# A message-passing layer on one core: filters made in one pass by PE, edges in the rows, without a bias pass on ACT and without transposes

## What is computed

```python
h = jnp.maximum(_layernorm(x, axis=-1), 0.0)
W = silu(dist_feat @ fw1 + fb1) @ fw2 + fb2      # one row of filters per edge
xt = silu(h @ aw1 + ab1) @ aw2 + ab2             # one row per node
msg = W * xt[src]
agg = jax.ops.segment_sum(msg, dst, num_segments=h.shape[0])
out = silu(agg @ ow1 + ob1) @ ow2 + ob2
return x + h + out
```

## Time and profile before

| | us |
|---|---|
| median of 3 runs | 2037.55 (2035.7 to 2040.6) |
| span of the profiled execution | 2356.9 |
| PE, DVE busy in it | 1290.8, 1191.7 |
| ACT, POOL busy in it | 520.7, 1526.1 |
| mean granted clock of PE | 0.741 of 2.4 GHz |

### The profile page before, as it was taken

The page is one execution under the profiler, slowest core; times in us unless marked ns, Lnnn a source line. Parts: engine busy times, 40 slices in busy tenths (PEclk is TensorE's granted clock), DMA queues, the critical chain, the costliest instruction groups (busy, mean ns, idle before and its releaser), DMA issues.

```text
span 2356.9 us, 13198 instructions
## 1 busy us (share of the span) xinstructions
PE 1290.8 (55%) x4526; PEld 700.7 (30%) x4526; DVE 1191.7 (51%) x1497; ACT 520.7 (22%) x545; POOL 1526.1 (65%) x1619
## 2 busy tenths in 40 slices
PE   3454555655565557555655565555564566554645
PEld 2222333332232323223322232222232233322323
DVE  4455445555455445544544564445444454444545
ACT  3322222222121122122212221222121122121211
POOL 5556666667666666666666666666666676666665
PEclk9686777777786768776877786777686777677867
DMA  4421222212221212212212221222221222212211
GB/s 148 144 76 45 82 58 71 79 51 85 82 83 45 83 50 81 87 46 81 86 51 78 80 85 50 80 65 65 82 85 48 82 54 81 85 45 82 59 46 44
DMA packets 62293, 171.47 MB, mean 73 GB/s; under 512 B 27088, under 2 KB 29648, under 8 KB 59024
## 3 DMA queue, kind: packets, MB, share of 16 engines
q0 software_dynamic: 51584, 105.75, 16.8%
q1 hardware_dynamic: 8192, 61.32, 6.9%
q10 hardware_dynamic: 2448, 3.54, 0.4%
HBM read 164.08 MB, written 6.42 MB: 72 GB/s over the span
## 4 chain that ended last, share of the span: by engine, by line
another core or an unknown queue 30%; POOL 24%; PE 18%; issue 16%; ACT 9%; DVE 2%; DMA 0%; SPq 0%; POOLq 0%; ACTq 0%; DVEq 0%
POOL xg L381 24%; PE banks L884 9%; PE banks L876 4%; ACT hid L444 4%; ACT hid L450 4%; PE banks L891 2%; PE banks L824 1%; PE banks L899 1%; ACT hs L469 0%; DVE stats L557 0%; PE banks L819 0%; DMA xs<-in_x 0%; PE banks L944 0%; DVE sums L668 0%
## 5 line engine op out<-in xcount | busy, mean ns | idle before, releaser
L381 POOL DMA_INDIRECT xg<-node_table,src x1564 | 1479.0, 946 | 777.6 <-issue 451.3
L884 PE MATMUL banks<-hid,wts 128*128 128x512 f32 x806 | 534.4, 798 | 556.3 <-ACT hid L444 437.9
L665 DVE TENSOR_TENSOR banks<-banks,xg 128x1024 f32<-128x1024 f32 (+1 forms) x198 | 241.4, 1219 | 1070.2 <-DMA xg<-node_table,src 607.2
L668 DVE TENSOR_REDUCE sums<-banks 128x128 f32<-128x1024 f32 (+1 forms) x408 | 494.0, 1211 | 13.7
L876 PE MATMUL banks<-attr,wts 50*128 50x512 f32 x806 | 284.4, 786 | 383.1 <-ACT hid L450 206.4
L444 ACT ACTIVATE hid<-banks,cols 128x1024 f32<-128x1024 f32 x202 | 224.7, 1112 | 887.9 <-remote 672.4
L450 ACT ACTIVATE hid<-banks,cols 128x1024 f32<-128x1024 f32 x202 | 224.6, 1112 | 865.6 <-remote 376.6
L884 PEld LDWEIGHTS banks<-hid,wts 128*128 128x128 f32 x806 | 180.6, 249 | 746.6 <-ACT hid L444 465.7
L891 PE MATMUL banks<-ident,hid 128*128 128x128 f32 x1612 | 283.5, 333 | 40.1 <-issue 38.1
L891 PEld LDWEIGHTS banks<-ident,hid 128*128 128x128 f32 x1612 | 224.6, 170 | 237.1 <-issue 228.6
L672 DVE TENSOR_TENSOR banks<-banks,other 128x1024 f32<-128x1024 f32 (+1 forms) x204 | 248.7, 1219 | 7.0
(11 more groups left out here) (83 smaller groups left out, 282.9 us busy)
## 6 DMA issues: line engine op xcount, KB each, us to landing
attr<-in_attr SPq DMA_DIRECT2D x25, 2048.0 KB
xg<-node_table,src POOLq DMA_INDIRECT x1564
out<-res ACTq DMA_DIRECT2D x8, 256.0 KB
xs<-in_x SPq DMA_DIRECT2D x3, 512.0 KB, 6.6
node_table<-res SPq DMA_DIRECT2D x3, 512.0 KB
out<-res ACTq DMA_DIRECT2D x5, 192.0 KB
spare<-in_dst SPq DMA_DIRECT2D x1, 808.0 KB
src<-in_src SPq DMA_DIRECT2D x1, 808.0 KB
```

The costliest lines, as they stand in the source:

```text
L381: pool.indirect_dma_start(xg[:, i % XG, j, :], None, table[:, :], bass.IndirectOffsetOnAxis(ap=src[:, s * L + j:s * L + j + 1], axis=0))\
L665: dve.tensor_tensor(to, to, rows_of, ALU.mult).then_inc(signal, 1)
L668: return dve.reduce_sum(sums[:, at, m, :], of.rearrange("p j f -> p f j"), AX.X)
L884: i = pe.matmul(hid_ps[:, at], w["fw2_s"][:, :], hid[:, s % 2, at], start=True, stop=True)
```

## The change

PE makes the filters with the edges in the partitions at once: the silu result is the stationary operand, `fw2` the moving one, eight matmuls of 128 columns a pair. fb2 comes from two bf16 matmuls of 512 columns ahead of them, which spread three bf16 parts of fb2 (`fb2_rows`) over the partitions. ACT's pass L450 and the transposes are gone, and `hid_ps` is written once a pair. DVE makes the parts of fb2 at its start, ahead of the statistics; before, that was part of a branch that isn't taken with these inputs. `hidden` runs two pairs ahead (FILL = 2). PE's semaphores of the loop (three raised a turn, and those of the steps) become one, `pe_turn`, raised by the last matmul of `hidden`; whoever waited for filters, transposes or steps of a turn waits for `hidden(s + 2)`, the last thing in PE's turn s ahead of the sums and the steps. POOL waits for it too.

```diff
+FILL = 2
+def after(s):
+    return run(s + FILL)
...
                 if i >= XG:
-                    pool.wait_ge(fil_done, run(s - REACH))
+                    pool.wait_ge(pe_turn, after(s - 1))
...
             def silu_hid(s):
                 n = tiles_in(s) * P
-                act.wait_ge(hid_sum, run(s))
+                act.wait_ge(pe_turn, run(s))
...
-            def add_fb2(s):
-                n = tiles_in(s) * P
-                act.wait_ge(across, run(s))
-                act.activation(hid[:, s % 2, 0:n], hid_ps[:, 0:n], ACT.Identity, bias=cols[:, 3:4]).then_inc(biased, 1)
...
             def pair(s):
-                for a in ((0, 1) if s == 0 else (s + 1,)):
+                for a in range(FILL + 1) if s == 0 else (s + FILL,):
                     if a < PAIRS:
                         silu_hid(a)
-                        add_fb2(a)
...
+            dve.wait_ge(s_rows, 16)
+            dve.wait_ge(s_set, 1)
+            dve.tensor_copy(fb2_part[:, 0, :], rows[:, 0, :]).then_inc(s_fb2, 1)
+            dve.wait_ge(s_fb2, 1)
+            dve.tensor_tensor(fb2_rest[:, 0, :], rows[:, 0, :], fb2_part[:, 0, :], ALU.subtract).then_inc(s_fb2, 1)
...
+            for i in range(3):
+                dve.tensor_copy(fb2_rows[32 * i:32 * i + 1, :, :],
+                                fb2_part[32 * i:32 * i + 1, i:i + 1, :].to_broadcast([1, TPG, F])).then_inc(s_fb2, 1)
...
-                dve.wait_ge(fil_done, run(s))
+                dve.wait_ge(pe_turn, after(s))
...
                 if s > 0:
-                    pe.wait_ge(biased, run(s - 1))
+                    pe.wait_ge(hid_done, run(s - 1))
...
-                i.then_inc(hid_sum, 1)
+                i.then_inc(pe_turn, 1)
...
             def filters(s):
+                to, halves = fil_ps[s % 2], range(tiles_in(s) // TPG)
+                pe.wait_ge(red_done, run(s, LAG))
+                for h in halves:
+                    pe.matmul(to[:, GC * h:GC * h + GC], ones_b[:, :], fb2_rows.rearrange("p j f -> p (j f)"), start=True, stop=False)
                 pe.wait_ge(hid_done, run(s))
-                for h in range(tiles_in(s) // TPG):
-                    at = slice(GC * h, GC * h + GC)
-                    i = pe.matmul(hid_ps[:, at], w["fw2_s"][:, :], hid[:, s % 2, at], start=True, stop=True)
-                i.then_inc(across, 1)
-
-
-            def by_edge(s):
                 for j in range(tiles_in(s)):
                     at = slice(j * P, (j + 1) * P)
-                    i = pe.transpose(fil_ps[s % 2][:, at], hid[:, s % 2, at], ident[:, :])
-                i.then_inc(fil_done, 1)
+                    i = pe.matmul(to[:, at], hid[:, s % 2, at], w["fw2_s"][:, :], start=False, stop=j % TPG == TPG - 1)
+                return i
...
             def pair(s):
                 if s == 0:
-                    hidden(s)
-                    filters(s)
-                if s + 1 < PAIRS:
-                    hidden(s + 1)
+                    for a in range(FILL):
+                        hidden(a)
+                i = filters(s)
+                if s + FILL < PAIRS:
+                    hidden(s + FILL)
                 else:
-                    pe.wait_ge(biased, run(s))
-                pe.wait_ge(red_done, run(s, LAG))
-                by_edge(s)
-                if s + 1 < PAIRS:
-                    filters(s + 1)
+                    i.then_inc(pe_turn, 1)
                 for a in SUMS_AT.get(s, ()):
                     pair_sums(a)
```

More of the change, by code:

```diff
@@ L150, in table_writes, with turn_of @@
     return sum(len(transfers(i)) for i in range(c + 1))
+def turn_of(kind, n, step):
+    return TASKS[TASK_OF[kind, n]][2] + (EARLY_STEPS if kind == "early" else OUT_STEPS)[step]
 def turns(pair, task):
@@ L287, in gnn_layer @@
         e_gathered = [sem(f"e_gathered{r}") for r in range(EARLY_PAIRS)]
-        hid_sum, hid_done, across, biased, fil_done, oh_done, msg_done, masked, first_done, red_done, half_msg, half_first, half_masked, half_red, win_done, group_done = (
-            sem(n) for n in ("hid_sum", "hid_done", "across", "biased", "fil_done", "oh_done", "msg_done", "masked", "first_done", "red_done", "half_msg",
+        pe_turn, hid_done, oh_done, msg_done, masked, first_done, red_done, half_msg, half_first, half_masked, half_red, win_done, group_done = (
+            sem(n) for n in ("pe_turn", "hid_done", "oh_done", "msg_done", "masked", "first_done", "red_done", "half_msg",
                              "half_first", "half_masked", "half_red", "win_done", "group_done"))
-        n_relu, n_tr, n_hT, n_l1, n_mid, n_l2, n_rows = (
-            sem(n) for n in ("n_relu", "n_tr", "n_hT", "n_l1", "n_mid", "n_l2", "n_rows"))
+        n_relu, n_hT, n_mid, n_rows, last_l1, last_l2 = (
+            sem(n) for n in ("n_relu", "n_hT", "n_mid", "n_rows", "last_l1", "last_l2"))
         r_din, r_key, r_in, r_gat, r_l1, r_hid, r_fil, r_msg, r_one, r_win, r_add, r_taken = (
@@ L328, in pair @@
                     if s >= 2 * PART:
-                        sp.wait_ge(hid_sum, run(s - PART - 1))
+                        sp.wait_ge(pe_turn, run(s - PART - 1))
                     at = s % (2 * PART) * GC
@@ L398, in _ @@
             act.dma_start(cols[:, :], cols_t).then_inc(s_cols, 16)
-            for ahead in (s_h, s_mid, a_mid, hid_done, biased):
+            for ahead in (s_h, s_mid, a_mid, hid_done):
                 act.sem_inc(ahead, AHEAD)
@@ L463, in task @@
                     if n >= 2:
-                        act.wait_ge(n_tr, n - 1)
+                        act.wait_ge(pe_turn, after(turn_of("early", n - 2, "copied")))
                     if n == 0:
@@ L473, in task @@
                     width, bias = (GC, 1) if kind == "early" else (OUTS[n][1] * P, 2)
[L474 to L477, removed]
+                    last = kind == "out" and n == len(OUTS) - 1
+                    if last:
+                        act.wait_ge(last_l1, 1)
+                    else:
+                        act.wait_ge(pe_turn, after(turn_of(kind, n, "middle")))
+                    source = last_ps_1 if last else node_ps
                     act.activation(mid[:, 0:width], source[:, 0:width], ACT.Silu, bias=cols[:, bias:bias + 1])\
@@ L551, in _ @@
             dve.memset(fb2_rows[:, :, :], 0.0).then_inc(s_set, 1)
+            dve.wait_ge(s_rows, 16)
[3 more added lines that the diff above has]
+            dve.tensor_tensor(fb2_rest[:, 0, :], rows[:, 0, :], fb2_part[:, 0, :], ALU.subtract).then_inc(s_fb2, 1)
+            dve.wait_ge(s_fb2, 2)
+            dve.tensor_copy(fb2_part[:, 1, :], fb2_rest[:, 0, :]).then_inc(s_fb2, 1)
+            dve.wait_ge(s_fb2, 3)
+            dve.tensor_tensor(fb2_rest[:, 1, :], fb2_rest[:, 0, :], fb2_part[:, 1, :], ALU.subtract).then_inc(s_fb2, 1)
+            dve.wait_ge(s_fb2, 4)
+            dve.tensor_copy(fb2_part[:, 2, :], fb2_rest[:, 1, :]).then_inc(s_fb2, 1)
+            dve.wait_ge(s_fb2, 5)
+            for i in range(3):
+                dve.tensor_copy(fb2_rows[32 * i:32 * i + 1, :, :],
+                                fb2_part[32 * i:32 * i + 1, i:i + 1, :].to_broadcast([1, TPG, F])).then_inc(s_fb2, 1)
             for k, (first, last) in enumerate(STAT_PARTS):
@@ L733, in task @@
                 if step == "copied":
-                    dve.wait_ge(n_tr, n + 1)
+                    dve.wait_ge(pe_turn, after(turn_of(kind, n, "copied")))
                     dve.tensor_copy(hT[:, 0:GC], node_ps).then_inc(n_hT, 1)
                 elif step == "rows" and kind == "early":
-                    dve.wait_ge(n_l2, b + 1)
+                    dve.wait_ge(pe_turn, after(turn_of(kind, n, "rows")))
                     dve.tensor_tensor(e_x[:, n * TPG:(n + 1) * TPG, :], node_ps.rearrange("p (j f) -> p j f", f=F),
@@ L747, in task @@
                     if to is yc:
-                        dve.wait_ge(n_l2, b + 1)
+                        dve.wait_ge(pe_turn, after(turn_of(kind, n, "rows")))
                     dve.tensor_tensor(to, to, rows[:, 2:3, :].to_broadcast([P, tiles, F]), ALU.add).then_inc(s_xs, 1)
                     if to is xc:
-                        dve.wait_ge(n_l2, b + 1)
+                        dve.wait_ge(last_l2, 1)
                     if n >= 2:
@@ L764, in _ @@
                     dve.wait_ge(s_out[i], 16 * len(OUTS[i::2]))
[L765 to L778, removed]
                 dve.sem_inc(r_msg, 1)
@@ L810, in _, with transposes @@
         def _(pe):
-            def transposes(to, b, n_tiles, signal):
+            def transposes(to, b, n_tiles):
                 for j in range(n_tiles):
                     i = pe.transpose(to[:, j * P:(j + 1) * P], hs[:, b, j, :], ident[:, :])
-                i.then_inc(signal, 1)
+                return i
             def layer1(source, n_tiles, weights, summed):
@@ L836, in node_transposes @@
                 pe.wait_ge(s_hT, run(c, 1))
-                transposes(tr_ps, b, TILES[c], s_tr)
+                transposes(tr_ps, b, TILES[c]).then_inc(s_tr, 1)
```

(20 more changed lines are left out.)

12 lines of the change are left out of this document (5 added, 7 removed).

## The result

The changed kernel takes 2049.59 us (median of 4 runs, 2048.06 to 2051.16) where before takes 2038.88 (4 runs, 2035.7 to 2040.6): the ratio is 1.0053, with a 95% interval of 1.0039 to 1.0066. It is 10.7 us slower.

The account below looks back on a forecast made before the run. POOL's 1612 gathers at 1.25 us, 2015 us, were taken as the bound; 2037.55 us plus 12 (early pairs), 3.0 (start) and 1.1 (node stage) gave 2053.6 us, range 2036 to 2068.

Parts of the forecast that it names:

- The bound and the mechanism: Main loop: POOL's gathers every 1.25 us, 2015 us in all, bound the kernel; PE's longer chain costs only where POOL waits.
- The early pairs' term: Six early pairs, which take no gather: POOL waits 2.0 us each for PE's longer chain, 12 us (2.7 to 23).
- PE needed only the transposes there: Kernel before, early pairs: transposes at half clock take 2.25 us with POOL's release, so no wait before the change.
- PE's 3.75 us: Early pair E: time left for PE between DVE's end with pair E-2, at 16.25, and gather E+1, due at 20.0.
- gather E+2: The gather for the second pair after early pair E: adds no wait once gather E+1's has been paid.
- The start: Gather 3 waits for turn 2, behind DVE's late end with pair 0: 3.0 us lost (1.0 to 5.4).
- The node stage: DVE's extra small passes ahead of the statistics delay the table and POOL's start in the pairs: 1.1 us (0 to 2.6).
- The account of the stalls: POOL's waits in the first profile of before, 321 us, come from profiling; without the profiler POOL hardly waits.
- the rival that they are: "Faster": stalls also occur in ordinary runs and partly vanish with PE's increments, 1845 to 2018 us; chance 0.10.
- Same: Early turns: PE at full clock and a slightly shorter chain make the six waits vanish, 2037 to 2041 us; chance 0.27.
- Slower still: Ordinary turns exceed their 13.75 us for PE; a tenth of them losing 2 us each gives 2094 us; chance 0.03.
- The full price of 3.85 us an early pair: Early pairs: upper end of each wait, with PE's whole burst at half clock, 7.6 us; 23 us in all.

Follow-up runs that it names:

- The direct waits of POOL: POOL waits for DVE's end with the pair that last used the slot, not for PE: changed kernel 2030.42 us, kernel before 2030.29 us.
- the chains shortened step by step: Changed kernel with POOL released by the filters instead of hidden, 2040.21 us; changed kernel without the bias matmuls for fb2, 2044.54 us.
- the run with two more increments: Changed kernel plus two more PE semaphore increments a turn that nobody waits for, three a turn as before: 2046.34 us, ratio 1.0048.
- the second profile of before: The kernel before, unchanged, profiled again: one run, 2036.49 us, with a span of 2034.7 us.

## Why the prediction held, and where it was off

**The bound and the mechanism: right.** POOL's spacing of 1.25 us is the clock of this kernel, ordinary turns cost nothing, the early pairs are where PE's longer chain comes too late. The direct waits of POOL show it from one side, the chains shortened step by step from the other.

**The early pairs' term: right in kind, two errors that nearly cancel against each other.** I had 2.0 us each, 12 in all, against nothing before. Four of the six were as forecast, 1.7 to 2.0. The clock was as argued, half at first and risen on the way: at the six pairs the filters ran at a granted clock of 0.51 to 0.54 and hidden at 0.87 to 1.00. But at 50 and 92 the changed kernel waited 4.7 and 4.6, and before had 3.3 at the same two. The step that failed is "PE needed only the transposes there": I did not follow what stands in PE's queue ahead of them. In turns 49 and 91 that is an output task's first matmul, held by the wait for DVE's rows until DVE's row pass is over, later than the moment from which I counted PE's 3.75 us; in before hidden stands between it and the transposes as well. The net term is 17.2 - 6.6 = 10.6, not 12. That it came so near is luck: what I left out added 5 us after the change and 6.6 before it. And 2.0 was picked between 0.45 and 3.85, not worked out.

Two smaller steps of that term were off as well. I priced the chain at full clock at 4.2 us; at pair 114 of the run with two more increments it took 3.5 with the 0.28 until POOL goes on, and the wait was 0.16 us, not 0.45. And gather E+2, to which I gave nothing, waited 0.8 us in all after the change. In the run with two more increments it waited 1.4 us at each of the two places where gather E+1 had hardly waited.

**The start: wrong, 3.0 forecast, 0 measured.** I took DVE's end with pair 0, 27.8 us after the first main gather, from a profile whose node stage was stalled. Undisturbed, the first main gather follows at once on the last early one. In the second profile of before it starts at 63.99 and DVE ends pair 0 at 87.58, 23.6 us later. After the change it starts at 64.68, and DVE ends pair 0 at 89.03:

```profile
64.68 0.94 POOL L393 DMA_INDIRECT xg<-node_table,src  x1 [0.30 <-issue]
...
87.81 1.22 DVE L691 TENSOR_REDUCE sums<-banks 128x128 f32<-128x1024 f32 x1
...
94.67 0.94 POOL L393 DMA_INDIRECT xg<-node_table,src  x1 [0.30 <-issue]
```

That is 24.4 us, so turn 2 has 5.6 us instead of 2.2, and gather 3 starts on its time, 30.0 us after the first and not 33.

**The node stage: 0 instead of 1.1, by an overlap that I had not seen.** DVE's extra passes delayed its statistics by 2.0 us (start at 9.74 instead of 7.69 in the second profile of before). By the end of the stage the delay was larger than I had allowed: DVE's last pass over the table's rows starts at 59.16 instead of 54.93, 4.2 us later. But POOL issues its 48 early gathers until then, and the table's last landing comes before the last of these, so they cover it:

```profile
8.79 0.91 DVE L574 COPY fb_rows<-fb_part 1x512 bf16<-1x512 bf16 x3
...
9.74 4.73 DVE L581 BATCH_NORM_STATS2 stats<-xs 128x6 f32<-128x128 f32 x24
...
59.16 0.96 DVE L595 TENSOR_TENSOR res<-banks,rows 128x768 f32<-128x768 f32 x1 [3.57 <-DMA node_table<-res]
...
63.44 0.94 POOL L381 DMA_INDIRECT e_x<-in_x,e_src  x1 [0.30 <-DMA node_table<-res]
```

The cover is thin: without the bias matmuls the table came 0.8 us too late in the profiled execution. I had taken the wait of 9.8 us for the table as the order of things; it was part of the stalls.

**The account of the stalls: right for the sum, wrong in its reason.** That the stalls aren't in the ordinary runs is confirmed: in 31 further runs of before the span lay between 2033.5 and 2039.2 us. So the rival that they are is dead. But I put them down to the profiler, and that fell: in each of the nine later profiles the span is 1.8 to 1.9 us below that same execution's time. One execution of before was disturbed, and what disturbed it stays open. Three increments a turn of PE don't bring it about by themselves, since neither the second profile of before nor the changed kernel with three shows it.

**What became of the rivals.** "Same" needed PE at full clock in the early turns, and it was not: the filters there took 3.38 to 3.55 us. Its argument was sound, though, for where PE did run at full clock, at pair 114 of the run with two more increments, gather 115 waited only 0.16 us. "Slower still" would have needed ordinary turns to run out of time; none did. The rule on idle gaps between bursts of matmuls (the Trainium skill, TensorE: Matmul & The Clock Gate, "Why this matters for your kernels") warns that the clock falls in such gaps. The trace agrees for the start of the burst: after 3.44 us of idling the filters at pair 30 took 3.46 us, which take 1.95 at full clock. That the whole burst would then run at half clock was my reading of it, and that did not hold: hidden took 1.13 to 1.28 us, near its full clock price. The full price of 3.85 us an early pair was reached nowhere without the task's step in front.

## What to carry to other kernels

When one engine's stream of issues is the bound, look at nothing but what it waits for: a wait should name the event that truly frees its resource, not a later one that happens to imply it. Going through PE cost this kernel 6.7 us before and 17 after the change; the direct wait gives both back in one line, and makes two very different PE programs equally fast. Where a pipeline skips an entry (a pair without a gather), every lag that is counted in turns loses a whole period there, and a slack that looks ample in the steady state must be recomputed for that place, with everything that is queued ahead on the waiting engine.

## What the runs showed of the hardware

- An indirect DMA that gathers 128 rows of 512 bytes costs POOL 1.25 us from start to start wherever it waits for nothing: the mean was 1.248 or 1.249 us in nine profiles and 1.250 in the disturbed one, and no single one was above 1.38. From the end of a pair's last record to DVE's start on the rows it was 1.5 to 1.7 us in 172 of the first 194 gathered pairs of the changed kernel's profile; in the others, the first aside, up to 5.4 us.
- A profiled execution can be 322 us longer than another of the same program (2356.9 and 2034.7 us of span) with the lengths of its instructions unchanged, by engines that go on late after PE: at POOL's 80 remote waits 2 to 16 us after the end of the last transposes. The busy times of DVE, ACT and POOL agree within 0.3% between the two, PE's within 3% (1290.8 and 1325.4 us, at a mean clock of 0.741 and 0.765). Its waits can't be used, until the span has been held against the time.
- Eight float32 matmuls of 128 columns with fresh weights each, sixteen records, cost PE 1.95 us at full clock (granted 1.00) and 3.62 at half (0.51); two of 512 columns, four records, cost about as much, 1.98 and 3.78. Timeline of the changed kernel, and of the kernel before in its first profile:

```profile
570.48 1.95 PE L898 MATMUL banks<-wts,hid 128*128 128x128 f32 x16
...
1395.49 3.62 PE L898 MATMUL banks<-wts,hid 128*128 128x128 f32 x16
```

```profile
117.18 1.98 PE L884 MATMUL banks<-hid,wts 128*128 128x512 f32 x4 [0.19 <-issue]
```
